# Attention block on one core: the rank-3 bias products replaced by tables added on GpSimd

## The reference

```python
mod = (_silu(L0_c) @ L0_wmod).reshape(8, 6, 1, -1)
sa, ca, ga, sb, cb, gb = (mod[:, 0], ..., mod[:, 5])
ga = (2 * (ga >= 0) - 1) * jnp.maximum(jnp.abs(ga), 0.25)      # gb alike
h = _layernorm(x) * (1 + ca) + sa
x = x + ga * attn(h)
...
def attn(x):
    Q, K, V = x @ Wq.T + bq, x @ Wk.T + bk, x @ Wv.T + bv      # 16 heads of 16
    Q, K = _rope(Q, pos), _rope(K, pos)                        # pairs turned by position
    scores = where(causal, Q K^T / 4, -1e9)
    return concat(softmax(scores) @ V) @ Wo.T + bo
```

## Time and profile before

| | us |
|---|---|
| three runs, median (lowest to highest) | 979.06 (978.99 to 983.0) |
| the profiled execution | 983.58 |
| its span | 981.8 |
| TensorE busy | 798.8 (81%) |
| VectorE busy | 625.9 (64%) |
| ScalarE busy | 481.2 (49%) |
| GpSimd busy | 295.0 (30%) |

### The profile page before, as it was taken

How to read it: one execution, slowest core, us unless ns; L and a number is a source line. 1 busy time by engine, 2 the same in 40 slices (tenths; PEclk the granted TensorE clock), 3 DMA queues, 4 the chain that set the end, 5 groups by cost and what they waited for, 6 DMA issues and landing times. The chain is left out here.

```text
span 981.8 us, 21339 instructions
## 1 busy us (share of the span) xinstructions
PE 798.8 (81%) x7674; PEld 503.2 (51%) x7674; DVE 625.9 (64%) x1192; ACT 481.2 (49%) x886; POOL 295.0 (30%) x377
## 2 busy tenths in 40 slices
PE   5859999999999999999886377401899999999895
PEld 3434445444444444444333177401777777777774
DVE  4747878888888878878661488794344444443442
ACT  1325666666666666666663055681433433334332
POOL 4203323323323323323221233473032322223221
PEclk9959999999999999999997565555899999999998
DMA  6152000100101001010100577772022221222100
GB/s 196 46 129 64 23 2 1 56 11 2 65 2 66 1 13 54 1 44 2 43 2 21 175 221 232 183 229 79 23 85 67 72 72 52 73 60 63 60 16 1
DMA packets 48527, 63.95 MB, mean 65 GB/s; under 512 B 9028, under 2 KB 42925, under 8 KB 48304
## 3 DMA queue, kind: packets, MB, share of 16 engines
q1 hardware_dynamic: 43440, 45.80, 15.5%
q0 software_dynamic: 4992, 16.81, 5.7%
HBM read 52.71 MB, written 17.73 MB: 72 GB/s over the span
## 5 line engine op out<-in xcount | busy, mean ns | idle before, releaser
L791 DVE TENSOR_REDUCE row_max<-ps_max 128x2 f32<-128x1024 f32 (+2 forms) x192 | 200.0, 1042 | 58.7 <-PE ps_max L460 56.0
L652 ACT ACTIVATE prob<-ps_sc 128x1024 f32<-128x1024 f32 (+1 forms) x192 | 169.2, 881 | 116.4 <-PE ps_sc L487 113.9
L313 POOL TENSOR_SCALAR_AFFINE_SELECT prob<-prob 128x512 f32<-128x512 f32 x128 | 84.0, 656 | 310.6 <-ACT prob L652 310.5
L1418 PE MATMUL ps_h<-tok_t,w_hi 128*128 128x128 f16 x1248 | 146.6, 223 | 22.0 <-issue 21.2
L1489 DVE CAST hid_hi<-hid 128x512 f16<-128x512 f32 x78 | 35.5, 455 | 170.4 <-ACT hid L1470 167.5
L1418 PE MATMUL ps_h<-tok_t,w_lo 128*128 128x128 f16 x624 | 128.4, 222 | 0.0
L1418 PEld LDWEIGHTS ps_h<-tok_t,w_hi 128*128 x1248 | 97.3, 99 | 45.5 <-issue 32.3
L1470 ACT ACTIVATE hid<-ps_h,b_t 128x128 f32<-128x128 f32 x312 | 88.7, 371 | 59.4 <-PE ps_h L1418 59.4
L101 POOL DMA_INDIRECT slots<-row_dram,token x39 | 40.1, 1027 | 199.8 <-DVE y L1501 185.1
L500 PE MATMUL ps_pv<-prob,v_sb 128*32 128x512 f32 (+3 forms) x1024 | 97.2, 453 | 0.0
L1461 ACT ACTIVATE tok_t<-ps_x 128x512 f16<-128x512 f16 x39 | 23.3, 597 | 134.1 <-PE ps_x L1403 134.1
(11 more groups left out here) (221 smaller groups left out, 1449.3 us busy)
## 6 DMA issues: line engine op xcount, KB each, us to landing
raw<-w SPq DMA_DIRECT2D x32, 512.0 KB, 4.9
xs<-x SPq DMA_DIRECT2D x8, 512.0 KB, 4.7
xr<-x SPq DMA_DIRECT2D x8, 512.0 KB, 3.9
row_dram<-gates_dram SPq DMA_DIRECT2D x1, 4096.0 KB
row_dram<-xr SPq DMA_DIRECT2D x8, 512.0 KB, 3.4
x<-row_dram SPq DMA_DIRECT2D x8, 512.0 KB, 4.5
row_dram<-rows SPq DMA_DIRECT2D x8, 512.0 KB, 4.3
prob<-wmod SPq DMA_DIRECT2D x1, 1536.0 KB, 8.4
```

What stands on the lines that cost most here:

```text
L313: nc.gpsimd.affine_select(out=diag, in_=diag, compare_op=ALU.is_ge, fill=0.0, base=0, pattern=[[0, HG], [1, P]], channel_multiplier=-1).th ...
L652: nc.scalar.activation(p_kb[:, :, first * L:(first + n) * L], ps_sc[:, :, 0:n * L], ACT.Exp, scale=SCALE).then_inc(exp_done, 1)
L791: nc.vector.tensor_reduce(dst, ps_max[:, :, 0:n * L].rearrange("p j (m l) -> p j m l", m=n), AX.X, ALU.max).then_inc(max_done, 1)
L1418: last = mm(o, w[:, :, k, f, :][:, bass.ds(e, 1), :].rearrange("p e m -> p (e m)"), tok_t[:, j % 2, part, k, :], start=(n == 0 and f % HF ...
```

## The change

- `bias3`, `ones3`, the splitting of the biases and the three products with ones are gone. Each accumulation now starts with its first product of weights.
- The biases of queries and keys are broadcast to all partitions (bias_qk). GpSimd turns them once for each of the four positions of a tile in its batch (`turn_bias`, the table rot_bias), and `rotate` adds the table in a second sum.
- `bv` and `bo` become one row for a batch: `constant_row` multiplies `bv` with the output weights, `keep_gates` adds `bo` and multiplies with the gate. The row goes out and comes back with the gates (gated_bias, one megabyte), and GpSimd adds it to x in `add_const`, between two of the clears.

```diff
@@ SP
-            for n, b_ in enumerate((bq, bk, bv, bo)):
-                sp.dma_start(bias_f[n * BR // 4:(n + 1) * BR // 4, :], b_.rearrange("(a n) -> a n", n=64)).then_inc(bias_loaded, 16)
...
-            sp.wait_ge(bias_split, 3)
-            for n in range(3):
-                sp.dma_start(bias3[n:n + 1, :].rearrange("a (r e) -> a r e", e=64), bias_parts[:, n, :]).then_inc(bias_spread, 16)
+            for n, b_ in enumerate((bq, bk)):
+                sp.dma_start(bias_qk[:, n * D:(n + 1) * D], b_.partition_broadcast(P)).then_inc(bias_loaded, 16)
+            sp.dma_start(bv_t[:, :], bv.rearrange("(c p) -> p c", p=P), allow_slow_non_contiguous=True).then_inc(bias_loaded, 16)
+            sp.dma_start(bo_rows, bo.partition_broadcast(B)).then_inc(bias_loaded, 16)
...
+            sp.dma_start(gated_bias[:, :, :].rearrange("p b d -> p (b d)"), gates_dram[2].partition_broadcast(P)).then_inc(gates_loaded, 16)
@@ GpSimd
-                nc.gpsimd.tensor_tensor(rot[:, :], rot_a[:, :], rot_b[:, :], ALU.add).then_inc(rot_done, 1)
+                nc.gpsimd.tensor_tensor(rot[:, :], rot_a[:, :], rot_b[:, :], ALU.add).then_inc(rot_summed, 1)
+                pool.wait_ge(rot_summed, T + 1)
+                nc.gpsimd.tensor_tensor(rot[:, :], rot[:, :], rot_bias[:, t, :], ALU.add).then_inc(rot_done, 1)
...
+            def turn_bias(t):
+
+                heads = bias_qk[:, :].rearrange("p (h d) -> p h d", d=DK)
+                spare = rot[:, :]
+                nc.gpsimd.tensor_tensor(spare.rearrange("p (h d) -> p h d", d=DK), heads,
+                                        cos_t[:, t, None, :].to_broadcast([P, 2 * H, DK]), ALU.mult).then_inc(bias_turned, 1)
...
+                for e in range(2):
+                    nc.gpsimd.tensor_tensor(turned[:, :, :, e], pairs[:, :, :, 1 - e],
+                                            sines[:, None, :, e].to_broadcast([P, 2 * H, DK // 2]), ALU.mult).then_inc(bias_turned, 1)
+                pool.wait_ge(bias_turned, 4 * t + 3)
+                nc.gpsimd.tensor_tensor(rot_bias[:, t, :], rot_bias[:, t, :], spare, ALU.add).then_inc(bias_turned, 1)
+                pool.wait_ge(bias_turned, 4 * t + 4)
+
+            def add_const(X):
+
+                par, t = place(X)
+                if t == 0:
+                    pool.wait_ge(xr_loaded[par], 16 * (X // (2 * QT) + 1))
+                if X == 0:
+                    pool.wait_ge(gates_loaded, 32)
+                nc.gpsimd.tensor_tensor(xr[:, par, t, :], xr[:, par, t, :], gated_bias[:, X // QT, :], ALU.add).then_inc(const_added, 1)
...
             rstd_of(0)
+            pool.wait_ge(bias_loaded, 64)
+            pool.wait_ge(rope_loaded, 32)
+            turn_bias(0)
             rstd_of(1)
+            for t in range(1, QT):
+                turn_bias(t)
...
                 clear_future(U, 1)
+                if U >= QT - 2 and U - QT + 2 < NT:
+                    add_const(U - QT + 2)
                 clear_future(U, 2)
                 clear_future(U, 3)
+            for X in range(NU - QT + 2, NT):
+                add_const(X)
@@ TensorE
-                    mm(ps, ones3[:, :], bias3[:, 0:2 * D], start=True, stop=False)
-                last = mm(ps, h_t[:, k, :], w_qkv[:, k, 0:2 * D], start=False, stop=(k == KC - 1))
+                last = mm(ps, h_t[:, k, :], w_qkv[:, k, 0:2 * D], start=(k == 0), stop=(k == KC - 1))
...
-                mm(ps[:, 0:D], ones3[:, :], bias3[:, 2 * D:3 * D], start=True, stop=False)
...
-                mm(o, ones3[:, :], bias3[:, 3 * D:4 * D], start=True, stop=False, skip_group_check=True)
...
+            def constant_row(ps):
+
+                pe.wait_ge(wt_kept, 4)
+                pe.wait_ge(bv_spread, 1)
+                for k in range(KC):
+                    last = mm(ps[0:B, 0:D], bv_all[:, k, :], w_o[:, k, :], start=(k == 0), stop=(k == KC - 1))
+                last.then_inc(const_ps, 1)
...
                     raw_gates(ps_nd)
+                    constant_row(ps_max[:, 1, :])
@@ VectorE
-            dve.wait_ge(bias_loaded, 64)
-            for n in range(3):
-                nc.vector.tensor_copy(bias_parts[:, n, :], bias_f[:, :]).then_inc(bias_split, 1)
...
+                dve.wait_ge(const_ps, 1)
+                link(nc.vector.tensor_tensor(mod_c, ps_max[0:B, 1, 0:D], bo_rows, ALU.add))
+                nc.vector.tensor_tensor(mod_c, mod_c, mod_r[:, 0, :], ALU.mult).then_inc(gates_done, 1)
...
+                dve.wait_ge(const_added, X + 1)
                 nc.vector.tensor_tensor(xr[:, par, t, :], xr[:, par, t, :], gated[:, :], ALU.add).then_inc(x1_done, 1)
...
-            dve.wait_ge(gates_loaded, 16)
+            dve.wait_ge(gates_loaded, 32)
```

More of the change, by code:

```diff
@@ L151, in attention_part @@
         sin_t = sb("sin_t", [P, QT, DK])
-        bias3 = sb("bias3", [3, 4 * D], BF16)
-        ones3 = sb("ones3", [3, P], BF16)
+        bias_qk = sb("bias_qk", [P, 2 * D])
+        rot_bias = sb("rot_bias", [P, QT, 2 * D])
+        bv_t = sb("bv_t", [P, KC])
+        bv_all = sb("bv_all", [P, KC, B])
+        gated_bias = sb("gated_bias", [P, B, D])
         tri_w = sb("tri_w", [P, 2, P], BF16)
@@ L169, in attention_part @@
         c_t = prob[:, 1, 1280:1280 + KC * B].rearrange("p (c b) -> p c b", c=KC)
-        mod_r = prob[0:B, 1, 1536:1536 + 2 * D].rearrange("p (g d) -> p g d", g=2)
-        mod_s = prob[0:B, 1, 2048:2048 + 2 * D].rearrange("p (g d) -> p g d", g=2)
-        mod_m = prob[0:B, 1, 2560:2560 + 2 * D].rearrange("p (g d) -> p g d", g=2)
-        BR = 4 * D // 64
-        bias_f = sb("bias_f", [BR, 64])
-        bias_parts = sb("bias_parts", [BR, 3, 64], BF16)
+        mod_all = prob[0:B, 1, 1536:1536 + 3 * D].rearrange("p (g d) -> p g d", g=3)
+        mod_r, mod_c = mod_all[:, 0:2, :], mod_all[:, 2, :]
+        mod_s = prob[0:B, 1, 2304:2304 + 2 * D].rearrange("p (g d) -> p g d", g=2)
+        mod_m = prob[0:B, 1, 2816:2816 + 2 * D].rearrange("p (g d) -> p g d", g=2)
+        bo_rows = prob[0:B, 1, 3328:3328 + D]
         x_v = x.rearrange("b (t p) d -> b p t d", p=P)
@@ L280, in _ @@
                                         pattern=[[-1, P]], channel_multiplier=1).then_inc(idents_done, 1)
-            nc.gpsimd.memset(ones3[:, :], 1.0).then_inc(consts_done, 1)
             nc.gpsimd.memset(neg_half[:, :], -0.5).then_inc(consts_done, 1)
@@ L417, in project_v @@
                 ge(pe, kt_kept, kept_before)
-                mm(ps[:, 0:D], ones3[:, :], bias3[:, 2 * D:3 * D], start=True, stop=False)
                 for k in range(KC):
-                    last = mm(ps[:, 0:D], h_t[:, k, :], w_qkv[:, k, 2 * D:3 * D], start=False, stop=(k == KC - 1))
+                    last = mm(ps[:, 0:D], h_t[:, k, :], w_qkv[:, k, 2 * D:3 * D], start=(k == 0), stop=(k == KC - 1))
                 last.then_inc(v_ps, 1)
@@ L527, in project_out @@
                 o = ps_nd[:, KC * P:KC * P + D]
-                mm(o, ones3[:, :], bias3[:, 3 * D:4 * D], start=True, stop=False, skip_group_check=True)
                 for k in range(KC):
-                    last = mm(o, att_t[:, k, :], w_o[:, k, :], start=False, stop=(k == KC - 1), skip_group_check=True)
+                    last = mm(o, att_t[:, k, :], w_o[:, k, :], start=(k == 0), stop=(k == KC - 1), skip_group_check=True)
                 last.then_inc(o_ps, 1)
+            def constant_row(ps):
[4 more added lines that the diff above has]
+                last.then_inc(const_ps, 1)
             x_transposes(0, ps_pv)
-            pe.wait_ge(consts_done, 8)
-            pe.wait_ge(bias_spread, 48)
+            pe.wait_ge(consts_done, 7)
             pe.wait_ge(wt_kept, 3)
@@ L558, in _ @@
             x_transposes(LEAD, ps_nd)
-            pe.wait_ge(consts_done, 24)
+            pe.wait_ge(consts_done, 23)
             for s in range(NSHOT):
@@ L730, in keep_gates @@
                 link(nc.vector.tensor_scalar(mod_m, mod_m, ADA_MIN, None, ALU.max))
-                nc.vector.scalar_tensor_tensor(out=mod_r, in0=mod_s, scalar=-1.0, in1=mod_m, op0=ALU.add,
-                                               op1=ALU.mult).then_inc(gates_done, 1)
+                link(nc.vector.scalar_tensor_tensor(out=mod_r, in0=mod_s, scalar=-1.0, in1=mod_m, op0=ALU.add, op1=ALU.mult))
+                dve.wait_ge(const_ps, 1)
+                link(nc.vector.tensor_tensor(mod_c, ps_max[0:B, 1, 0:D], bo_rows, ALU.add))
+                nc.vector.tensor_tensor(mod_c, mod_c, mod_r[:, 0, :], ALU.mult).then_inc(gates_done, 1)
             def statistics(T):
@@ L841, in _ @@
                     keep_modulation(3, ps_max[:, 0, :], 2)
+                    dve.wait_ge(bias_loaded, 64)
+                    nc.vector.tensor_copy(bv_all[:, :, :], bv_t[:, :, None].to_broadcast([P, KC, B])).then_inc(bv_spread, 1)
                 if T == 2:
```

23 lines of the change are left out of this document (12 added, 11 removed).

## The result

| | before | changed |
|---|---|---|
| median of the runs taken side by side, us | 979.83 (20 runs, 975.5 to 984.34) | 985.37 (20 runs, 982.62 to 986.89) |
| profiled execution, its span, us | 983.58, 981.8 | 983.31, 981.6 |
| TensorE busy, us | 798.8 | 770.6 |
| VectorE busy, us | 625.9 | 634.2 |
| GpSimd busy, us | 295.0 | 370.9 |

The changed kernel takes 1.0049 times the time of the one before (95%: 1.0035 to 1.0063), 5.5 us more, where 17.7 more were forecast. The ratios leave out runs in a slower state of the chip, of which there was one, a run of e9 at 1118 us.

A forecast was written before the change was run, and what follows sets the result against it. TensorE looked like the bound, but GpSimd's chain to weigh(U, 1) had only 0.4 us of room. Setup +15.8, units +2.3 and +1.6, end -2.0 sum to +17.7 us: 997 us on the median of 979.06, range 986 to 1006.

The forecast's parts named there:

- 1.9 for `constant_row` and `keep_gates`: Setup: `constant_row` adds 0.95 us on TensorE, two more VectorE steps of `keep_gates` with their waits add 0.95.
- The setup: Before the loop: turning the bias tables on GpSimd delays rotate(0) and what follows, +15.8 us (11 to 20).
- the clock's term: Setup: idle TensorE drops to the lower clock, slowing modulation(3), +1.7 us; bounds 0 and +3 (next projection slow too).
- The units: Attention loop: GpSimd takes what TensorE is given back, +0.10 us a unit for U = 4 to 26 (-0.2 to +0.35).
- the +2.3 of units 4 to 26 and the +1.6 of units 0 to 3: Loop totals in us: 23 units at +0.10 each; first four, GpSimd already last and no output product to save.
- +1.04 on GpSimd: Chain from rope to weigh(U, 1): second sum 1.26 plus wait 0.1, less 0.22 of rstd's wait and 0.1 of gaps.
- +0.31 at the maxima: Sixth shot of a unit: next maxima at 315.62 against 315.31, after a loss of 0.62 us waiting for the clear.
- The end: Units 27 to 31 and the four last outputs: no rotation, nine bias products of 0.2 to 0.3 saved, -2.0 us.
- The constant on GpSimd: Units: the 0.8 us sum into x fits between the clears of blocks 1 and 2; nothing (0 to +0.1 a unit).
- Rival 1: Units: second sum doesn't reach the path, each of 27 gains 0.6; 976 us; chance 0.08 including what lies up to 984.
- Rival 3: Contention: table tiles at the upper bound (+3.6 us) and 0.2 more in each of 27 units (+5.4), 1006 us; chance 0.12.
- What would have shown it wrong: First maxima before 69 us, small `prob` waits with units of 14.1, or waits there and units over 15.1.

The follow-up runs named there:

- e9: Changed kernel with the table added to rot_a while VectorE makes the sine products, leaving one sum behind VectorE: 978.79 us, ratio 0.9976 to the kernel before.
- e4: Kernel before without its three bias products and nothing in their place, all four biases left out: 960.29 us, ratio 0.9797.
- e5: Changed kernel with the table turned but never added, so only the first sum in the rotation: 978.45 us, ratio 0.9979 to the kernel before.
- e3: Changed kernel with the table cleared by one memset instead of turned, the second sum kept: 969.26 us, ratio 0.9886 to the kernel before.
- e6: Changed kernel with the next tile's rstd behind the clear of block 1, in the loop alone: 985.64 us, ratio 1.0063 to the kernel before.
- e12: Changed kernel without GpSimd's sum of gated_bias into x and the wait on it: 985.86 us, ratio 1.0047 to the kernel before.
- first profile: Original profiled execution of the kernel before, no edit: 983.58 us, span 981.8, one of its slowest runs.
- second profile: Kernel before profiled again without an edit: span 976.9 us; the runs' time was 980.23 us, ratio 1.0008.
- e2: Changed kernel with table tiles 1 to 3 turned one by one between the lead's rotations: 976.16 us, ratio 0.9958 to the kernel before.
- e11: e2 with tables 1 to 3 replaced by three memsets each in the same queue places: 976.73 us, ratio 0.9956 to the kernel before.
- e10: Changed kernel with e9's edit, masks first, table loads ahead of wmod, tiles 0 to 2 before rotate(0), last behind rotate(1): 968.44 us, ratio 0.9871 to the kernel before.

## Why the forecast missed

The runs nearly close the account. Products away -20 (e4), the second sum +7 (985.4 - 978.5, e5), the turning +16 (985.4 - 969.3, e3), together +3; the measured +5.5 leaves 2.5. The forecast had 1.9 for `constant_row` and `keep_gates`, but each of the three terms is known to about 2 us, and no run takes these two out alone, so how much of the 2.5 is theirs isn't shown.

- **The setup, +15.8 forecast: right in its steps.** rotate(0) at 37.3 forecast, 37.17 measured (38.3 to 38.4 in e5, e6 and e12, where the last bias came 1.1 us later); the last bias at 15.5 and 15.08; a table tile of 4.2 and 4.3; the transposes of tile 2 at 41 and 40.83; modulation(3) at 3.55 and 3.42; the first maxima at about 74 and 75.44. The loop's first rotation came 15.4 later than in the first profile and 17.0 later than in the second. That difference is the upper bound of the clock's term, "the next projection slow too": it took 3.65 us here and 1.98 in the second profile, but 3.51 in the first, on which the sum was worked. The bound taken for a product of 256 (0.81, by the line through the two rows) was met: 1.63 for two, 0.82 each. The one measurement of the Trainium skill ("GPSIMD Engine Reference", Performance versus the Vector engine: 4,497 ns for an add of 2,048) gave an estimate of 0.56 by a line through the origin; the rows disagree with that line at this size.
- **The units, +0.10 each forecast, -0.39 measured: this is the step that failed.** Over the 26 intervals that is +3.9 against -10.2 (the +2.3 of units 4 to 26 and the +1.6 of units 0 to 3): 14.1 us, somewhat more than the whole miss of 13.0 in the span, since the setup missed by 1.2 the other way. The mechanism was half right: the wait on the clear appears in nearly every unit, the second sum costs TensorE time, and what it costs comes off what the products give. Its size was wrong, and ScalarE's part in the sixth shot was not in the sum at all. There are three places, all found by laying both kernels against the unit's first scores, in an ordinary unit each.
  - First, the term "+1.04 on GpSimd". From the rotation's start to the clear's end it was 311.05 to 314.09, 3.04 us, and is 305.96 to 309.74, 3.78: +0.74. The added 1.35 (305.96 to 307.31) swallowed more than the 0.22 and 0.1 that were allowed: memset, rstd and clear now follow at 308.52, 308.59 and 309.10 without a gap, and the exponential for which the clear had waited 0.26 is done in time (it ends at 308.20). That 0.26 of idle time stood in the very row and was left out: 1.04 - 0.26 = 0.78. So `weigh(U, 1)` waits 0.30 and not 0.62, and against the first scores it comes 0.04 later.
  - Second, the scores of shot 5, the sixth, started 0.35 behind their maxima before (315.66 against 315.31), held by ScalarE's exponential of shot 4, which ended at 315.60 (rows below), and 0.24 behind them now, so against the first scores they come 0.08 earlier than they did. The forecast took TensorE and VectorE as level in this shot and didn't look at ScalarE.
  - Third, with the product of 0.21 the space around it went too, 0.07 more.

  From +0.31 at the maxima the forecast went to +0.10 at the unit's end; measured are +0.03 and -0.36. And every fourth unit was longer than the others by 0.38 before, and is by 0.13 now, which was not forecast at all: ScalarE's late copy of the values (e5) makes it long, and with the second sum the other three are held up in the same shot.

```profile
314.58 1.02 ACT L652 ACTIVATE prob<-ps_sc 128x1024 f32<-128x1024 f32 x1
...
315.66 0.29 PE L487 MATMUL ps_sc<-q_t,k_t 64*128 64x128 f16 x4
```

- **The end, -2.0 forecast**: -1.6 against the second profile, which is luck. In the changed kernel the last two output projections ran at the lower clock, in the second profile the last three, and that one projection at full clock makes the step between two outputs 3.08 us instead of 4.34, so 1.3 of the 1.6. Against the first profile it would be -4.5.
- **The constant on GpSimd at nothing: right** (e12); one of its sums takes 0.73 where 0.8 was forecast. In the lead `constant_row` took 0.96 and the two steps of `keep_gates` 0.41 each, as forecast.
- **Rival 1**, that the second sum doesn't reach the path, is half true. Its -0.6 a unit is just what e4 and e5 gain without the sum; with it, 0.25 of the 0.61 is lost in three units of four. Its 976 us needed a shorter chain by 0.6; it was shorter by 0.3.
- **Rival 3**, contention: the low part beside the constant's sum takes 0.61 instead of 0.415 (e12), which agrees with what the Trainium skill ("GPSIMD Engine Reference", Key points) says of VectorE instructions with two SBUF inputs, while the sum itself, 0.73, is no longer than where no low part runs. That costs no time in a unit. Contention shows in the lead of e2 too, where its price can't be told from that of the queue (e11), and hardly in the lead of the change itself: only xhat of tile 1 is longer there (1.35), at a time when GpSimd is what is late.
- What would have shown it wrong, as put there: waits small and units of 14.1, or waits there and over 15.1. The third case, waits there and units under 14.7, was not thought of. A wait that is seen says that a step is last, not how much later it is than what was last before.

## What to carry to other kernels

An engine's idle gaps inside a chain are slack that an added instruction eats first: before adding the instruction's length to a chain, subtract each "idle before" in the rows behind it, the ones with another engine's name too. Then look at every engine that waits for the chain, not at the busiest alone (e6: ScalarE). Where an added sum of two operands can take the one that is ready early, put it there (e9: the same instructions, 0.25 us in three units of four). And work that depends on inputs alone belongs into an engine's idle time of the setup, with its loads placed by what else waits for the queue (e10: of its 17 us some 10 come from that).

## What the hardware showed that was not expected

Some VectorE instructions with all operands in SBUF wait for a whole GpSimd instruction. Those with one input did so even beside a memset, which only writes: xhat took 0.41 us alone, 1.34 beside a product of 1.26 and 1.75 beside a memset of 1.70, and the copy of 16 numbers to `bv_all` 0.16, 0.65 and 1.58. The low parts, with two inputs, took 1.07 beside a product and 0.41 beside the memset. It goes both ways: the pair of 256 products, 1.63 in the changed kernel, took 1.88 in e2 while VectorE's low parts ran. In the steady units of the kernel before it was there already: xhat took 0.72 in three units of four, beside a clear of GpSimd, and 0.41 in the fourth, with none beside its start.
